# ScalarE's copies and Squares put behind its activations, and the head of a fused four-block convolution reordered

## The reference

```
h = relu6(bn1(conv1x1(x, tern(w1))))          # 32 -> 192 channels
h = relu6(bn2(conv3x3(h, tern(w2), pad 1)))   # 192 -> 192
x = x + bn3(conv1x1(h, tern(w3)))             # 192 -> 32
# then: two 3x3 convolutions of 32 channels with inputs and weights on 8-bit grids, bn, relu, residual
# then twice: y = relu(bn(conv3x3(x) + b)), channels with max|y| < 0.001 set to zero

tern(w): delta = 0.7 * mean|w|;  mask = |w| > delta
         alpha = sum(|w| * mask) / sum(mask);  result alpha * sign(w) * mask
```

## Time and profile before

| | us |
|---|---|
| median of 3 runs | 271.41 (271.15 to 271.43) |
| the profiled execution | 271.47 |
| its span | 269.5 |
| PE busy | 241.1 (89%) |
| VectorE busy | 242.5 (90%) |
| ScalarE busy | 195.2 (72%) |
| GpSimd busy | 11.5 (4%) |

### The profile page before, as it was taken

The page is one execution under the profiler, slowest core; times in us unless marked ns, Lnnn a source line. Parts: engine busy times, 40 slices in busy tenths (PEclk is TensorE's granted clock), DMA queues, the critical chain, the costliest instruction groups (busy, mean ns, idle before and its releaser), DMA issues.

```text
span 269.5 us, 5621 instructions
## 1 busy us (share of the span) xinstructions
PE 241.1 (89%) x2159; PEld 133.1 (49%) x2159; DVE 242.5 (90%) x473; ACT 195.2 (72%) x288; POOL 11.5 (4%) x30
## 2 busy tenths in 40 slices
PE   0649989998999989899999999999988999889992
PEld 0315554555554545455555555455534555445541
DVE  5799799999999999999999999899878858999894
ACT  5799876977756886777467868888433738998962
POOL 4800000000000000000000000000000000000003
PEclk9999999999999999999999999999999999999998
DMA  7528100200012000002100000000000000275306
GB/s 233 101 55 238 44 1 15 77 0 0 2 37 55 1 2 1 2 0 67 26 0 4 0 0 2 0 4 0 2 0 1 2 0 0 62 154 108 87 21 238
DMA packets 7098, 11.09 MB, mean 41 GB/s; under 512 B 2176, under 2 KB 5216, under 8 KB 7072
## 3 DMA queue, kind: packets, MB, share of 16 engines
q1 hardware_dynamic: 6880, 10.69, 14.9%
q10 hardware_dynamic: 192, 0.04, 0.1%
HBM read 4.04 MB, written 1.61 MB: 21 GB/s over the span
## 4 chain that ended last, share of the span: by engine, by line
DVE 44%; PE 23%; ACT 16%; issue 12%; DMA 2%; SPq 1%; DVEq 0%; ACTq 0%
PE ps L462 6%; ACT hs L783 5%; PE ps L639 5%; DVE hs L1149 4%; DVE ug L1142 4%; ACT ra L761 4%; PE ps L493 4%; PE ps L472 4%; DVE vv L1167 3%; DVE vv L1160 3%; PE ps L482 2%; DMA big<-w2b_in 2%; DVE ps L1188 2%; DVE vv L1166 2%; ACT big L968 2%
## 5 line engine op out<-in xcount | busy, mean ns | idle before, releaser
L761 ACT ACTIVATE ra<-ps,bn 128x392 f32<-128x392 f32 x64 | 42.6, 673 | 21.9 <-PE ps L440 20.9
L783 ACT ACTIVATE hs<-ug,magic 128x784 f16<-128x784 f16 x32 | 30.3, 952 | 17.7 <-DVE ug L1142 17.6
L472 PE MATMUL ps<-vv,w2at 128*128 128x392 f16 x192 | 37.9, 333 | 0.0
L462 PE MATMUL ps<-vv,wu 128*128 128x392 f16 x180 | 35.5, 332 | 0.0
L676 PE MATMUL ps<-big,wst 128*32 128x392 f16 (+2 forms) x576 | 25.6, 333 | 3.5 <-DVE big L1484 1.9
L440 PE MATMUL ps<-xk,w1t 96*128 96x392 bf16 x60 | 20.2, 348 | 9.0 <-ACT ra L761 5.4
L639 PE MATMUL ps<-qi,wqi 128*128 128x392 bf16 (+2 forms) x144 | 25.0, 333 | 0.7 <-ACT qi L936 0.7
L472 PEld LDWEIGHTS ps<-vv,w2at 128*128 128x128 f16 x192 | 18.4, 97 | 13.0 <-issue 1.0
L462 PEld LDWEIGHTS ps<-vv,wu 128*128 128x128 f16 x180 | 17.4, 97 | 11.0
L676 PEld LDWEIGHTS ps<-big,wst 128*32 128x32 f16 x576 | 14.8, 96 | 14.4 <-DMA big<-big 2.7
L472 PE MATMUL ps<-vv,w2bt 128*128 128x392 f16 x96 | 21.5, 333 | 0.0
(11 more groups left out here) (215 smaller groups left out, 428.3 us busy)
## 6 DMA issues: line engine op xcount, KB each, us to landing
xk<-xpart SPq DMA_DIRECT2D x45, 49.0 KB, 1.9
xin<-x_in SPq DMA_DIRECT2D x4, 392.0 KB, 3.8
big<-part SPq DMA_DIRECT2D x25, 56.2 KB, 2.0
big<-big SPq DMA_DIRECT2D x3, 450.0 KB, 3.9
y_out<-xin SPq DMA_DIRECT2D x3, 392.0 KB, 2.4
big<-w2a_in SPq DMA_DIRECT2D x3, 288.0 KB, 4.5
big<-w2b_in SPq DMA_DIRECT2D x6, 144.0 KB, 4.6
y_out<-xin SPq DMA_DIRECT2D x2, 196.0 KB, 2.3
```

The costliest lines, as they stand in the source:

```text
L462: i = nc.tensor.matmul(ps[:, PBANK[k], :HALF], weights(s, k, dx, False), moving(s, k, dx, b), start=(s == 0 and dx == 0), stop=(s == 2 and ...
L472: i = nc.tensor.matmul(ps[:, PBANK[k], :HALF], weights(s, k, dx, False), moving(s, k, dx, b), start=False, stop=(s == 2 and dx == 2), skip ...
L761: nc.scalar.activation(dst[:, HALF * h:HALF * h + HALF], ps[:, bank, :HALF], ACT.Relu, bias=bn[:, BSH, at:at + 1], scale=bn[:, BSC, at:at ...
L783: nc.scalar.activation(inner(hs[:, 2 * two]), img(ug[:, two, :]), ACT.Identity, bias=magic[:, 2:3]).then_inc(hh_ready, 1)
```

## The change

In words, with the names of the functions:

- SP waits until all of w2b has landed, loads w2b to partitions 64 to 127, and then w3 (before: w3, then that load, with no wait).
- PE: the eight filler products ahead of the last third of image 0's middle products are gone. In slot (0, 0) total(4) is issued after middle(1, 1) and not ahead of expand(2, 1), and expand(2, 3) after middle(2, 1) and not ahead of it.
- ScalarE, head: the Square of w2at comes directly behind the Relu pass of w2a, and so ahead of the activations of image 1; the Square of w2bt goes into slot (0, 0), behind relu_exp(2, 0); x_high(1, 0) goes behind slot (0, 0).
- ScalarE, slots: x_high stands behind relu_exp(j+2, 2), directly ahead of coarse(j+2, 0); x_high(2, 0) and x_high(3, 0), which stood between slots, are in the slots (0, 2) and (1, 2). The first integer_block of the slots (3, 0) and (3, 1) moves in the same way.

```diff
@@ block.sync
+            sp.wait_ge(s_w2b, 48)
+            for k in range(3):
+                dy = slice(3 * HID * k, 3 * HID * k + 3 * HID)
+                sp.dma_start(w2br[HB:P, dy], w2b[:, dy]).then_inc(s_w2c, 16)
             sp.dma_start(w3r[:, 0, :], w3[0:P]).then_inc(s_w3, 16)
             sp.dma_start(w3r[0:HB, 1, :], w3[P:HID]).then_inc(s_w3, 16)
             sp.dma_start(w3r[HB:P, 1, :], w3[P:HID]).then_inc(s_w3, 16)
-            for k in range(3):
...
@@ block.tensor, slot
                 if begin:
                     outer(3, j, b)
-                    pe.wait_ge(a_sum, 4)
-                    total(4, 2, ...)
...
                 middle(1, j + 1, b1)
                 if begin:
+                    pe.wait_ge(a_sum, 4)
+                    total(4, 2, ...)
                     expand(j + 2, 2)
-                if ahead:
+                elif ahead:
                     expand(j + 2, 3)
                 middle(2, j + 1, b1)
+                if begin:
+                    expand(j + 2, 3)
@@ block.tensor, head
                 if s == 2:
-                    warm(8)
                     pe.wait_ge(w2_ready, 3)
@@ block.scalar, slot
                 if begin:
                     copy_y(j)
                     relu_exp(j + 2, 0)
+                    act.wait_ge(w2_ready, 3)
+                    act.wait_ge(a_sum, 3)
+                    nc.scalar.activation(wjunk[0:HB, :], w2bt..., ACT.Square, accum_out=...).then_inc(a_sum, 1)
...
-                if split is not None:
-                    x_high(split, 1)
-                if after is not None:
-                    integer_block(after, 0)
                 if ahead:
                     relu_exp(j + 2, 1)
                     relu_exp(j + 2, 2)
+                if split is not None:
+                    x_high(*split)
+                if after is not None:
+                    integer_block(after, 0)
@@ block.scalar, head
             nc.scalar.activation(ajunk, ajunk, ACT.Relu, ...).then_inc(a_sum, 1)
+            act.wait_ge(a_sum, 1)
+            nc.scalar.activation(ajunk, w2at..., ACT.Square, accum_out=...).then_inc(a_sum, 1)
             for quarter in range(4):
                 relu_exp(1, quarter, bank=(0, 1, 5, 6)[quarter])
...
-            x_high(1, 0)
-            (both Squares, with their waits)
             copy_m1(0)
...
-            slot(0, 1, first=True, split=1)
-            x_high(2, 0)
-            slot(0, 2, first=True)
-            slot(0, 3, first=True, split=2)
+            x_high(1, 0)
+            slot(0, 1, first=True, split=(1, 1))
+            slot(0, 2, first=True, split=(2, 0))
+            slot(0, 3, first=True, split=(2, 1))
...
-            x_high(3, 0)
-            slot(1, 2)
-            slot(1, 3, split=3)
+            slot(1, 2, split=(3, 0))
+            slot(1, 3, split=(3, 1))
```

More of the change, by code:

```diff
@@ L292, in _ @@
             sp.dma_start(w3r[HB:P, 1, :], w3[P:HID]).then_inc(s_w3, 16)
-            for k in range(3):
-                dy = slice(3 * HID * k, 3 * HID * k + 3 * HID)
-                sp.dma_start(w2br[HB:P, dy], w2b[:, dy]).then_inc(s_w2c, 16)
             def spread(c):
@@ L524, in slot @@
                     outer(3, j, b)
-                    pe.wait_ge(a_sum, 4)
-                    total(4, 2, col[:, PART1 + 1:PART1 + 5:3], col[:, PART2 + 1:PART2 + 5:3])
                 if ahead:
@@ L534, in slot @@
                 if begin:
+                    pe.wait_ge(a_sum, 4)
+                    total(4, 2, col[:, PART1 + 1:PART1 + 5:3], col[:, PART2 + 1:PART2 + 5:3])
                     expand(j + 2, 2)
-                if ahead:
+                elif ahead:
                     expand(j + 2, 3)
                 middle(2, j + 1, b1)
+                if begin:
+                    expand(j + 2, 3)
                 if last and g == G - 2:
@@ L819, in slot @@
                     relu_exp(j + 2, 0)
+                    act.wait_ge(w2_ready, 3)
+                    act.wait_ge(a_sum, 3)
+                    nc.scalar.activation(wjunk[0:HB, :], w2bt[0:HB].rearrange("p t o -> p (t o)"), ACT.Square,
+                                         accum_out=col[0:HB, PART2 + 4:PART2 + 5]).then_inc(a_sum, 1)
                 else:
@@ L871, in _ @@
                                  accum_out=col[:, PART1 + 1:PART1 + 2]).then_inc(a_sum, 1)
+            act.wait_ge(a_sum, 1)
+            nc.scalar.activation(ajunk, w2at[:].rearrange("p t o -> p (t o)"), ACT.Square,
+                                 accum_out=col[:, PART1 + 4:PART1 + 5]).then_inc(a_sum, 1)
             for quarter in range(4):
```

## The result

| us | median | lowest to highest | runs |
|---|---|---|---|
| before | 271.32 | 271.15 to 272.58 | 6 |
| after | 269.06 | 268.86 to 269.22 | 6 |

The ratio is 0.990, with an interval of 0.988 to 0.993: about 2.3 us faster, where 2.6 were forecast (268.8, range 267.8 to 270.5). The profiled execution after took 269.16 (before 271.47), with a span of 267.4 (before 269.5). So 2.1 us of the difference can be followed in the trace. Read at three places, it is 1.40 at scales(), 0.27 more up to the last slots, and 0.48 more in the tail, where 1.84, 0.17 and 0.6 were forecast.

A forecast was written before the change was run, and what follows sets the result against it. VectorE was taken as the bound from about 30 to 160 us, PE and ScalarE from 162. Gains 1.44 + 0.4 + 0.17 + 0.6 = 2.6 us gave 268.9 profiled, 268.8 median, range 267.8 to 270.5.

The forecast's parts named there:

- Part 1: Head: moving ScalarE's Squares and dropping PE's eight fillers gains 1.66 us, less 0.22 waiting for the count: 1.44.
- Part 2: Loads: holding w2c and w3 back until w2b has landed brings 0 to 0.77 us, taken as 0.4.
- Rival (a): Loads: w2b lands no earlier, so the gain is 2.2 us and the time 269.2; chance 0.28.
- Part 3: Slots: x_high copies behind the activations end the wait of residual(1, 0) for PE's project, gaining 0.17 us.
- Rival (d): Slots: x_high copies delay coarse and so VectorE, up to 3.75 us against 2.6 gained: slower, 272.6; chance 0.06.
- Part 4: Tail, slots (3, 0) and (3, 1): integer_block behind the activations ends two PE stalls; 0.6 us arrives, bounds 0.3 to 0.84.
- (b): Head's wait is replaced, VectorE takes only 0.6 of 1.66, tail gives 0.3: 1.1 us, 270.3; chance 0.14.
- (c): Whole change brings nothing measurable, 271.4: the head's chain hangs on something the waits misattribute; chance 0.06.

The follow-up runs named there:

- fillers_back: The changed kernel with the eight filler products back ahead of the last third of image 0's middle products: 270.48 us, ratio 0.997.
- squares_back: The changed kernel with ScalarE's two Squares and x_high(1, 0) back ahead of copy_m1(0): 270.67 us, ratio 0.997.
- xhigh_back: The changed kernel with the x_high copies back ahead of relu_exp(., 1) and between slots: 269.60 us, ratio 0.993.
- set 3: Runs on one chip: changed kernel unaltered 270.02 us; with 12 fillers, not 18, 268.79; those 12 plus old load order 268.89, or plus early GpSimd edge memsets 268.27.

## Why the prediction was right or wrong

**Part 1, right.** In the profiled execution VectorE has no wait for c1a, and both halves of the edit are needed (fillers_back, squares_back). Products 1 and 2 of image 0 end at 27.08, where 27.05 was forecast, and c1a starts at 26.61, where 26.6 was. The count is late as forecast. By the distance from seeds to scales() it costs 0.51 (6.92 against 6.41), where 0.22 was forecast; 0.22 to 0.23 is what it costs in the five traces in which PE comes in time, so the forecast's own mechanism is met, and the other 0.28 is PE's lateness, which belongs to part 2. One statement beside it doesn't hold: without the removal of the fillers the gain was to be about 0.6. In fillers_back it is 0.66 at the seeds (28.46 against 29.12), but 0.12 at scales(), because the count, now behind middle(1, 1), is late by the fillers too.

**Part 2, the step that was mis-sized.** "An earlier landing can therefore bring 0 to 0.77, and everything up to 27.44 would shift with it. [...] I take 0.4". The landing was right: VectorE's sum starts at 9.12, 0.40 earlier. Over all traces it starts at 9.18 to 9.52 in the four with the old order and at 8.74 to 9.34 in the ten with the new (means 9.37 and 8.99). The ranges overlap, but on average w2b lands about 0.4 earlier when w3 and w2c are held back; what the prediction drew from the Trainium skill ("DMA: Bandwidth & Descriptors", section "Queues, rings and completion order"), that the landing wouldn't move, isn't borne out. What failed is that the gain arrives. The forecast has scales() at 35.53 - 1.84 = 33.69; they came at 34.13, and the 0.44 has two parts. First, line 1084 was held by GpSimd's memset, so the first activation came only 0.14 earlier (12.27 against 12.41), and even that is GpSimd's own, whose memset of part ended 0.13 earlier (12.01 against 12.14), not w2b's. The seeds came at 27.21, where 27.06 was forecast: 0.15. Second, the head's bound had become PE. The forecast for the count's end without the loads, 34.1, was met to 0.01, and it should have been 33.7 with them: PE got its input only 0.14 earlier (17.76 against 17.90), and the fillers took 0.18 more in this execution (4.65 against 4.47), so that the third product group started at 25.90, where it would have started at 25.85 before without the eight fillers. That is the other 0.29. Instead of 0.4 the loads brought 0.0 to 0.1. Rival (a) had this price for another reason: its 269.2 is nearer to the 269.06 than the forecast, but w2b did land earlier. No load was late by its move: VectorE doesn't wait ahead of lines 1126 and 1089 in the kernel after.

**Part 3, right, slightly larger.** residual(1, 0) no longer waits, and the shift grows from 1.40 to 1.67 there, 0.27 against a forecast of 0.17 (where nothing is waited for, VectorE starts the next instruction 0.09 ahead of the end of the one before, and this comes on top of the 0.17). xhigh_back gives 0.23 to 0.28 back. Rival (d), that a copy delays coarse, is out: ScalarE's idle time ahead of coarse(5, 0) grew from 0.33 to 1.61, by more than the copy's 0.75 (ScalarE's timeline after).

```profile
67.71 0.95 ACT L785 ACTIVATE hs<-ug,magic 128x784 f16<-128x784 f16 x1 [1.61 <-DVE ug L1141]
```

**Part 4, right, 0.48 against 0.6.** No stall on ra at 164 and 176 us, and outer(0, 14) starts at 183.07, 2.16 before the old 185.23, behind seeds that now start at 182.36; the forecast's reason for less than 0.84, VectorE's seeds, is where the rest stayed: their start moved by 1.67 and no more. TensorE's timeline after, for the earlier trace rows:

```profile
164.06 0.34 PE L441 MATMUL ps<-xk,w1t 96*128 96x392 bf16 x1
...
176.34 0.34 PE L441 MATMUL ps<-xk,w1t 96*128 96x392 bf16 x1
...
183.07 1.18 PE L473 MATMUL ps<-vv,w2at 128*128 128x392 f16 x6
```

The sum: 1.40 + 0.27 + 0.48 = 2.15 against 2.1 of the spans. Rivals (b) and (c) are out with the seeds at 27.21 and no wait for c1a. That the total came within 0.3 us of the forecast owes something to luck, because the prediction has no term for the pace of the 18 fillers, which its own edit makes count. In set 3 the same kernel had a median of 270.02, only 1.6 below the one before, and in its traced execution 0.83 of the 0.9 us it was longer lie in the head.

## What to carry to other kernels

When an edit makes an engine's unbroken work the bound, look again at what that work contains: fillers that were free under another wait are now paid for, and by a varying amount. A short instruction of unusual length in a timeline can be a wait that no view of waits names, so compare it with its neighbours and with what GpSimd does at that moment. And where times scatter by more than a term, read the term from the distance between the same instructions in two traces.

## What the hardware showed unexpectedly

- PE's clock doesn't rise at the same point in each execution of one kernel: 18 filler products took 4.65 us in one and 5.48 in another, both from 19.02, and over all traces with 18 of them 4.19 to 5.48. The granted clock of the windows reads 1.00 over 0.1 to 34 us all the same. The Trainium skill says so of slow products at the start ("TensorE: Matmul & The Clock Gate", section "What's actually happening": their number varies from run to run); the traces agree: the eleventh product started at 21.96 and the rest were fast in one, the sixteenth at 23.59 in the other. Between these two executions the whole time moved by 0.9 us (269.16 and 270.07).
- A strided memset on GpSimd, 128x448 in f16, takes 1.35 us, and a VectorE product of 128x2 elements that began within it took up to 0.94 (squares_back) instead of 0.22, while VectorE's next instruction ran on time. The 128x1 products at 11.15 and 11.34, within the same memset, kept their 0.15.
- Loads queued behind w2b (w3, and w2b once more to the other half of the partitions) delay its last landing on average: 5.3 to 5.7 us from issue in the four traces with them, 4.9 to 5.5 in the ten without.
